# Half of a folded weight product from scaled fp16 parts, and another order of the opening work on all engines

## The reference

```python
def _L0_gnn_ref(feature, graph, weight, wq, wk):
    output = jnp.einsum('bni,io->bno', feature, weight)
    q = jnp.einsum('bni,io->bno', feature, wq)
    k = jnp.einsum('bni,io->bno', feature, wk)
    alpha = jnp.einsum('bno,bmo->bnm', q, k)
    alpha = jnp.maximum(alpha, 0.0) * (graph != 0).astype(alpha.dtype)
    alpha = jax.nn.softmax(alpha, axis=1)
    return jnp.einsum('bnm,bmo->bno', alpha, output)
h = jnp.maximum(_layernorm(x, axis=-1), 0.0)
x = x + _L0_gnn_ref(h, adj, L0_gnn_weight, L0_gnn_wq, L0_gnn_wk)
```

## Time and profile before

| | us |
|---|---|
| median of 3 runs | 412.74 (412.74 to 412.88) |
| profiled execution | 412.91 |
| its span | 411.1 |
| TensorE busy | 405.3 |
| VectorE busy | 298.1 |
| ScalarE busy | 277.7 |
| GpSimd busy | 264.7 |

### The profile page before, as it was taken

The page is one execution under the profiler, slowest core; times in us unless marked ns, Lnnn a source line. Parts: engine busy times, 40 slices in busy tenths (PEclk is TensorE's granted clock), DMA queues, the critical chain, the costliest instruction groups (busy, mean ns, idle before and its releaser), DMA issues.

```text
span 411.1 us, 9529 instructions
## 1 busy us (share of the span) xinstructions
PE 405.3 (99%) x3580; PEld 321.7 (78%) x3580; DVE 298.1 (73%) x571; ACT 277.7 (68%) x592; POOL 264.7 (64%) x286
## 2 busy tenths in 40 slices
PE   8999999999999999999999999999999999999995
PEld 5444545979797997979798897979889797979884
DVE  5797789896867676776767777676777667656565
ACT  4749887765867677766777776776867777644534
POOL 0767896979495866759395775939577584910004
PEclk9999999999999999999999999999999999999999
DMA  8973858989889897997969498985978599493022
GB/s 284 373 110 67 217 103 217 232 205 217 181 208 191 245 155 212 189 204 188 192 212 196 156 214 199 197 218 173 198 241 158 156 220 181 75 197 112 2 104 102
DMA packets 161641, 75.03 MB, mean 183 GB/s; under 512 B 135360, under 2 KB 143808, under 8 KB 161600
## 3 DMA queue, kind: packets, MB, share of 16 engines
q1 hardware_dynamic: 161168, 73.81, 77.6%
q10 hardware_dynamic: 432, 0.66, 0.4%
HBM read 24.12 MB, written 16.78 MB: 99 GB/s over the span
## 4 chain that ended last, share of the span: by engine, by line
PE 90%; DVE 4%; DMA 2%; ACT 1%; SPq 1%; issue 1%; POOL 0%; DVEq 0%; POOLq 0%
PE bank L1166 10%; PE bank L1165 10%; PE bank L1163 10%; PE bank L1181 10%; PE bank L1180 10%; PE bank L1178 10%; PE s_bank L1192 3%; PE s_bank L1193 3%; PE s_bank L1194 3%; PE bank L1199 2%; PE bank L1200 2%; PE bank L1201 2%; PE bank L1320 2%; PE bank L1322 2%; PE bank L1321 2%; DMA x_sb<-in_x 2%
## 5 line engine op out<-in xcount | busy, mean ns | idle before, releaser
L423 POOL TENSOR_TENSOR hn_lo<-h,hn_hi 128x512 f16<-128x512 f32 x64 | 74.0, 1166 | 53.1 <-ACT hn_hi L554 52.9
L544 ACT ACTIVATE h<-x_sb,shift,rstd 128x512 f32<-128x512 f32 x64 | 50.0, 804 | 24.0 <-POOL shift L418 23.6
L449 POOL TENSOR_TENSOR hn_lo<-s,hn_hi 128x512 f16<-128x512 f32 x56 | 63.3, 1163 | 0.3 <-ACT hn_hi L559 0.3
L1163 PE MATMUL bank<-hT_hi,mt_hi 128*128 128x256 f16 x224 | 61.1, 273 | 0.0
L1165 PE MATMUL bank<-hT_lo,mt_hi 128*128 128x256 f16 x224 | 61.1, 273 | 0.0
L1180 PE MATMUL bank<-wt_lo,hT_hi 128*128 128x256 f16 x224 | 61.1, 273 | 0.0
L1166 PE MATMUL bank<-hT_hi,mt_lo 128*128 128x256 f16 x224 | 61.1, 273 | 0.0
L1178 PE MATMUL bank<-wt_hi,hT_hi 128*128 128x256 f16 x224 | 61.1, 273 | 0.0
L1181 PE MATMUL bank<-wt_hi,hT_lo 128*128 128x256 f16 x224 | 61.1, 273 | 0.0
L559 ACT ACTIVATE hn_hi<-s 128x512 f16<-128x512 f32 x56 | 33.8, 625 | 25.6 <-POOL s L438 19.9
L1180 PE MATMUL bank<-w_lo,hT_hi 128*128 128x256 f16 x168 | 45.8, 273 | 0.0
(11 more groups left out here) (169 smaller groups left out, 1115.2 us busy)
## 6 DMA issues: line engine op xcount, KB each, us to landing
out_h<-x_sb SPq DMA_DIRECT2D x63, 256.0 KB, 2.1
x_sb<-in_x SPq DMA_DIRECT2D x15, 1024.0 KB, 5.5
adj_sb<-in_adj SPq DMA_DIRECT2D x16, 256.0 KB, 5.3
hn_hi<-in_L_gnn_wq SPq DMA_DIRECT2D x4, 256.0 KB, 5.6
x_sb<-in_x SPq DMA_DIRECT2D x2, 512.0 KB, 7.2
w_sb<-in_L_gnn_weight SPq DMA_DIRECT2D x2, 512.0 KB, 8.7
hn_lo<-in_L_gnn_wk ACTq DMA_DIRECT2D x2, 256.0 KB, 3.8
hn_lo<-in_L_gnn_wk SPq DMA_DIRECT2D x2, 256.0 KB, 3.7
```

The costliest lines, as they stand in the source:

```text
L423: nc.gpsimd.tensor_tensor(hn_lo[:, s, b], h[:, b], hn_hi[:, s, b], ALU.subtract).then_inc(h_split, 1)
L449: nc.gpsimd.tensor_tensor(low, s32[:, f], high, ALU.subtract).then_inc(s_split, 1)
L544: nc.scalar.activation(h[:, b], x_sb[:, s, b], ACT.Relu, bias=shift[:, b:b + 1], scale=rstd[:, b:b + 1]).then_inc(h_made, 1)
L1163: nc.tensor.matmul(o, bh[:, k, cols], ah[:, :, k], start=first and c == 0 and k == 0, stop=False, skip_group_check=True)
```

## The change

Blocks 2 and 3 of M (`PARTS`) are no longer products in fp32. ScalarE makes the high parts of wk and of the last two blocks of wq, scaled by powers of two from their own maxima; GpSimd makes three of the four low parts of wk from an fp32 copy of the scaled values, VectorE the fourth and those of wq; TensorE multiplies the parts as it does elsewhere. So the maxima of wk, wq and weight are spread one after the other, in three steps each, in place of one spread for all three. v of graphs 0 to 2 is made in another order, part by part, with separate semaphores for the high and low transposes. On ScalarE the exponentials and high parts of p of group 0 go ahead of some high parts of h of group 2; on VectorE the low parts of t (blocks 2 and 3) go ahead of those of `wt`; the statistics and scale blocks of groups 1 and 2 are split or moved; the product with p waits for each graph.

```diff
-    SCALE_STEPS = 7
+    SCALE_STEPS = 12
+    KEY_SCALED, QUERY_SCALED, M_SCALED, W_SCALED = 3, 6, 7, 11
+    PARTS = (2, 3)
...
+        wk_hi, wk_lo = hn_lo[:, 1, 0:K], hn_lo[:, 1, K:2 * K]
+        wk_scaled = spare[:, 0:3].rearrange("p k a d -> p k (a d)")
+        wq_hi, wq_lo = (t[:, 0:2].rearrange("p f a d -> p f (a d)").rearrange("p f (k n) -> p f k n", k=K)
+                        for t in (mt_hi, mt_lo))
...
@@ def _(pool):
+            lo_of_wk(0)
+            lo_of_wk(1)
+            first_scales(0, 0)
+            lo_of_wk(2)
+            first_scales(0, 1)
             for b in range(GB):
                 lo_of_h(0, 0, b)
...
+            first_scales(1, 0)
...
-            layernorm_scales(1)
+            first_scales(1, 1)
             for b in range(GB):
                 lo_of_h(1, 1, b)
+            layernorm_scales(2)
...
-            layernorm_scales(2)
             pool.wait_ge(mt_summed, 3)
...
@@ def _(act):
+            act.wait_ge(scale_step, KEY_SCALED)
+            act.wait_ge(wkT_copied, K)
+            for k in range(K):
+                if k < 3:
+                    nc.scalar.activation(wk_scaled[:, k], wkT[:, k].rearrange("p r n -> p (r n)"), ACT.Copy,
+                                         scale=key_scale).then_inc(wk_scaled_made, 1)
+                nc.scalar.activation(wk_hi[:, k], wkT[:, k].rearrange("p r n -> p (r n)"), ACT.Copy,
+                                     scale=key_scale).then_inc(wk_hi_made, 1)
+            def hi_of_wq(r):
+                act.wait_ge(wqT_filled, r + 1)
+                act.wait_ge(scale_step, QUERY_SCALED)
+                nc.scalar.activation(wq_hi[:, r - 2], wT_bank[r % 2], ACT.Copy, scale=query_scale).then_inc(wq_hi_made, 1)
+            for r in PARTS:
+                hi_of_wq(r)
             for b in range(GB):
                 normalise_h(0, 0, b)
...
-            act.wait_ge(scale_step, 3)
+            act.wait_ge(scale_step, W_SCALED)
             for k in range(K):
...
             normalise_h(2, 2, 2)
+            exponentials(0)
             normalise_h(2, 2, 3)
+            hi_of_p(0)
...
             hi_of_h(2, 0, 2)
             hi_of_h(2, 0, 3)
-            exponentials(0)
-            hi_of_p(0)
...
@@ def _(vec):
+            for r in range(K):
+                key_max(r)
+            top(KEY)
+            query_max(0)
+            top_row(KEY, 0)
+            query_max(1)
+            power(KEY, 0, 0)
+            query_max(2)
+            query_max(3)
+            top(QUERY)
+            stats_first(0)
+            stats_first(1)
+            top_row(QUERY, 1)
+            power(QUERY, 1, KEY_SCALED)
+            stats_first(2)
+            stats_first(3)
+            nc.vector.scalar_tensor_tensor(m_scale[:], key_scale, M_BACK, query_scale, ALU.mult, ALU.mult).then_inc(scale_step, 1)
+            nc.vector.scalar_tensor_tensor(s_unscale[:], pow2[:, QUERY:QUERY + 1], 1.0 / (H_SCALE ** 2 * T_SCALE * m_factor),
+                                           pow2[:, KEY:KEY + 1], ALU.mult, ALU.mult).then_inc(scale_step, 1)
             for k in range(2):
                 vec.wait_ge(w_loaded[k], 16)
+                weight_max(w_sb[:, HK * k:HK * (k + 1)], w_max[:, W, HK * k:HK * (k + 1)])
+            top(W)
+            lo_of_wq(PARTS[0])
+            top_row(W, 2)
+            for r in PARTS[1:]:
+                lo_of_wq(r)
+            power(W, 2, M_SCALED + 1)
+            lo_of_wk(3)
             for k in range(K):
                 vec.wait_ge(w_hi_made, k + 1)
...
+            stats_all(1, 1, 0)
+            stats_all(1, 1, 1)
             for k in range(K):
                 vec.wait_ge(m_hi_made, k + 1)
...
+            stats_all(1, 1, 2)
+            stats_all(1, 1, 3)
...
+            lo_of_whole_t(0, 2)
+            lo_of_whole_t(0, 3)
             lo_of_wt(0)
             lo_of_wt(1)
-            lo_of_whole_t(0, 2)
-            lo_of_whole_t(0, 3)
...
@@ def _(pe):
             transpose_wq(0)
+            spread_top(KEY, 0)
             transpose_wq(1)
-            product_m(0)
+            spread_row(KEY, 0)
+            product_m(0, range(K - 1))
+            spread_top(QUERY, 1)
+            product_m(0, range(K - 1, K))
             transpose_wq(2)
             transpose_wq(3)
-            product_m(1)
...
+            spread_row(QUERY, 1)
+            for c in range(1, PARTS[0]):
+                product_m(c)
+            pe.wait_ge(wk_hi_made, K)
+            for c in PARTS:
+                pe.wait_ge(wq_hi_made, c - PARTS[0] + 1)
+                for k in range(K):
+                    scaled_m(c, wq_hi, wk_hi, k, start=k == 0)
+            spread_top(W, 2)
+            pe.wait_ge(wk_lo_pool, 3)
+            for c in PARTS:
+                for k in range(3):
+                    scaled_m(c, wq_hi, wk_lo, k)
+            spread_row(W, 2)
+            for c in PARTS:
+                pe.wait_ge(wq_lo_made, c - PARTS[0] + 1)
+                for k in range(K):
+                    scaled_m(c, wq_lo, wk_hi, k)
+            pe.wait_ge(wk_lo_vec, 1)
+            for c in PARTS:
+                scaled_m(c, wq_hi, wk_lo, 3, stop=True)
...
+            pe.wait_ge(hT0_hi_landed[0], 16)
+            for k in range(K):
+                pe.wait_ge(w_hi_made, k + 1)
+                first_v(0, hT_hi, w_hi, k, start=k == 0)
...
-            pe.wait_ge(p_split, GB)
             pe.wait_ge(scores_read, 1)
             for b in range(GB):
+                pe.wait_ge(p_split, b + 1)
                 product_out(0, b)
```

More of the change, by code:

```diff
@@ L157, in graph_attention_kernel @@
         shift = sb("shift", [N, GB], F32)
+        W, QUERY, KEY = range(3)
+        w_scale, key_scale, query_scale = (scale_of[:, i:i + 1] for i in (W, KEY, QUERY))
+        m_factor = W_TOP / (4 * D)
+        M_BACK = m_factor / 2.0 ** (2 * W_SHIFT)
         row_max = sb("row_max", [N, GB], F32)
@@ L1303, in product_m, with spread_top, spread_row, scaled_m @@
                     last.then_inc(m_filled, 1)
+            def spread_top(i, n):
+                pe.wait_ge(top_step, 2 * n + 1)
+                nc.tensor.transpose(top_bank[0:1, 0:N], w_top[:, i:i + 1], ident[:]).then_inc(top_filled, 1)
+            def spread_row(i, n):
+                pe.wait_ge(top_step, 2 * n + 2)
+                pe.wait_ge(consts_made, 5)
+                nc.tensor.matmul(top_bank[:, N:N + 1], ones[:], top_col[:, i:i + 1], start=True, stop=True).then_inc(top_filled, 1)
+            def scaled_m(c, left, right, k, start=False, stop=False):
+                mm = nc.tensor.matmul(M_BANK[c], left[:, c - 2, k], right[:, k], start=start, stop=stop)
+                if stop:
+                    mm.then_inc(m_filled, 1)
+            def first_v(b, left, right, k, start=False, stop=False):
+                mm = nc.tensor.matmul(v_bank(0)[b], left[:, 0, b, k], right[:, k], start=start, stop=stop)
+                if stop:
+                    mm.then_inc(whole_v, 1)
             def whole_product_v(g, b):
@@ L1343, in _ @@
-            pe.wait_ge(top_step, 3)
-            pe.wait_ge(consts_made, 5)
-            nc.tensor.matmul(top_bank[:, N:N + 3], ones[:], top_diag[:], start=True, stop=True).then_inc(top_filled, 1)
-            product_m(2, range(1, K))
-            product_m(3)
-            for b in range(GB - 1):
-                pe.wait_ge(hT0_landed[b], 2 * 16)
-                whole_product_v(0, b)
+            spread_row(QUERY, 1)
+            for c in range(1, PARTS[0]):
+                product_m(c)
+            pe.wait_ge(wk_hi_made, K)
@@ new lines, in _ @@
+            pe.wait_ge(wk_lo_vec, 1)
[5 more added lines that the diff above has]
+                first_v(0, hT_hi, w_hi, k, start=k == 0)
+            pe.wait_ge(hT0_lo_landed[0], 16)
+            for k in range(K):
+                first_v(0, hT_lo, w_hi, k)
+            pe.wait_ge(hT0_hi_landed[1], 16)
+            for k in range(K):
+                first_v(1, hT_hi, w_hi, k, start=k == 0)
@@ new lines, in _ @@
+            for k in range(K):
+                pe.wait_ge(w_split, k + 1)
+                first_v(0, hT_hi, w_lo, k, stop=k == K - 1)
+            for k in range(K):
+                first_v(1, hT_hi, w_lo, k)
+            pe.wait_ge(hT0_lo_landed[1], 16)
+            for k in range(K):
+                first_v(1, hT_lo, w_hi, k, stop=k == K - 1)
+            pe.wait_ge(hT0_hi_landed[2], 16)
+            for k in range(K):
+                first_v(2, hT_hi, w_hi, k, start=k == 0)
+            for k in range(K):
+                first_v(2, hT_hi, w_lo, k)
@@ L1353, in _ @@
+            pe.wait_ge(hT0_lo_landed[2], 16)
+            for k in range(K):
+                first_v(2, hT_lo, w_hi, k, stop=k == K - 1)
             pe.wait_ge(m_split, K)
```

167 lines of the change are left out of this document (87 added, 80 removed).

## The result

The change made the kernel slower: 414.04 us (median of 10 runs, 413.74 to 414.46) against 412.75 of the kernel before (10 runs beside them, 412.62 to 413.79), a ratio of 1.0029, 95% interval 1.0021 to 1.0037. Forecast were 411.85 us, with 411.4 to 413.1 as the range. The profiled execution took 413.76 us, its span is 411.9; before it was 412.91 and 411.1.

The account below looks back on a forecast made before the run. TensorE's own stream was taken as the bound, shortenable only up to 31.7 us. M 1.15, fourth product -0.45, vanished wait 0.31 made 1.0, less 0.1 for restarts: 412.74 to 411.85 us, range 411.4 to 413.1.

Parts of the forecast that it names:

- The sum of the head: TensorE's stream up to the first t product: 1.15 - 0.45 + 0.31 = 1.0 us gained, taken as 0.9.
- the fifth transpose: SyncE's transposes of h: the fifth lands at 27.7 us, TensorE asks at 28.1, so hidden by 0.4 us.
- The loss at the fourth product: First v products of graph 0: the fourth waits for ScalarE's high part of w, starting 23.6 not 23.15, 0.45 us lost.
- the 0.1 that I took off for restarts: TensorE's fp16 products behind the spreads of maxima: restarts shown in no row, 0.1 us taken off the 1.0 gain.
- B: Weight's scale on VectorE: one-column operations wait behind GpSimd's low parts of h, t 0.35 us later, 413.1 us; chance 0.15.
- E: SyncE's strict queue: fifth transpose one issue (1.31 us) later, 0.9 not hidden, gain gone, 412.75 us; chance 0.06.
- C: VectorE's two-tensor operations (low part of wk, scalings) miss their turn against GpSimd; gain only 0.3 to 0.6, 412.3 us; chance 0.20.
- D: Weight's spread earlier than listed, high parts of w in time: up to 0.45 us more gain, 411.4 us; chance 0.07.
- Behind it: After the first t product: earlier exponentials keep the 0.9 us gain; h of group 2 some 3 us late, costed at nothing.
- The cover: First product with p, near 57.9 us: moving exponentials ahead saves some 2 us; even half covers the 0.9 us lead.
- The scale block: GpSimd's scale block of group 2 ahead of M's sums: these end up to 1.63 us later; costed nothing, 0 to 0.3 in range.
- My last sentence: If t starts at 30.8 but the span has not shrunk by 0.9, a later wait took the gain; no chance given.

Follow-up runs that it names:

- experiment 5: The changed kernel with group 0's exponentials and GpSimd's scale block of group 2 both moved back to their old places; 412.95 us, ratio 1.0009 to the kernel before.

## Why the prediction was wrong

**The sum of the head was right.** M done at 22.29 (forecast 22.5), the weight's scale at 20.76 (21.0), the fourth v product at 23.41, released by w_hi (23.6), low parts of M in time, the fifth transpose landed at 25.9, ahead of its use at 27.95, and t at 30.54 (30.8). The common 0.2 to 0.3 us is the start: the first product of M at 8.12 (8.46), which is no fixed time: in the profile of experiment 5 it is 8.62. The loss at the fourth product was 0.45 in the forecast; it starts at 23.41 and could at 22.29 + 3 x 0.216 = 22.94, which is 0.47. The head gained 1.09 counted from M's first product, against 0.9; the 0.1 that I took off for restarts was not needed. (One sum was off: 21.0 + 3 x 0.61 + 0.71 is 23.54, not 23.57, which changes nothing.)

**None of the rivals B to E came.** VectorE's timeline of the changed kernel at the weight's scale:

```profile
20.42 0.15 DVE L1070 TENSOR_SCALAR pow<-w_top 128x1 int32<-128x1 int32 x1
20.61 0.15 DVE L1074 TENSOR_SCALAR scale_of<-pow 128x1 int32<-128x1 int32 x1
```

GpSimd made low parts of h meanwhile:

```profile
18.50 3.94 POOL L442 TENSOR_TENSOR hn_lo<-h,hn_hi 128x512 f16<-128x512 f32 x3 [0.30 <-ACT hn_hi L582]
```

An operation on one column of one tensor does not wait for it: 0.15 us, twice, both inside one operation of GpSimd (19.73 to 20.88), where three columns had taken 0.56. The Trainium skill (VectorE: DVE Perf Modes, Mode 2×_2P) asks of an operation that takes both read ports an outermost non-unit dimension that is even, or odd and equal in source and destination. Read strictly, that could cover one column too; the measurement decides against that reading. For C, TensorE has no idle time at 18.31; for D, the high parts of w still came late for the fourth product; for E, see the transpose above.

**The step that failed is "Behind it".** I costed the delay of the high parts of h of group 2 at nothing, since no wait of TensorE stood on it in the earlier trace rows. A table that shows no wait shows no slack either, and its idle time hid the wait of 0.19 us at 57.93. The slack was 0.26 us at the third p product of group 1, in rows that I did not read, and the sum needed two numbers against it: the delay that the move brings (0.87 by then) and the lead itself (1.39), which alone is larger. The delay of h was about what I wrote (3 us, measured 3.1 for the last high parts and 2.0 for the last h), and a part of it was absorbed; it was its price that was wrong: not 0, but 1.8 us when the move was made alone, and 2.0 at the third p product with the lead of the head against it. Without the move the rest of the change takes 411.98 us, close to the 411.85 that I forecast for the whole; but that sum had the scale block's sign wrong too, so its closeness is in part luck.

**The cover was not needed.** I let the move pay for the wait of 57.87 us. In the profile of experiment 5 the exponentials start at 50.77, 0.3 later than before, TensorE is 0.89 early, and the first p product, which now waits for one graph's part and not four, has no wait. The edit of the wait was enough.

**The scale block had the other sign.** I gave it 0 to 0.3 us of loss; it brings 0.8 to 1.2 (0.20 to 0.28%). Without it h of group 2 waits for its shift, on ScalarE ahead of the exponentials. I had looked at what it is moved past, the sums of M, and not at who waits for it.

My last sentence named this outcome, a start of t in time and a span that has not shrunk; no rival carried it, and no part of the range.

## What to carry over

When TensorE has no idle time, ask of each supplier how long before its use it is done; a gain ahead of that point is kept only up to the smallest of these distances, unless the suppliers come earlier too. Compare two timelines from an event that both have (here M's first product) and by starts: the span's first microseconds vary from one execution to the next, and idle time leaves out the overlap that is lost. A step moved ahead on an engine that works in order is priced by two rows: how long its own input is still out (here 1.94 us of standing), and what is queued behind it. Such a move is best tried alone, and a change of several moves one by one: here the gain hangs on one moved call (1.0009 without it), and the whole of the loss on another move.

## What the runs showed of the hardware

A four-column operation of GpSimd took 0.20 us in one order and 1.12 us in another, twice, and ended 0.06 us behind an operation of VectorE on two tensors (0.69 us) that had begun meanwhile; a delay of 0.9 us on the way to all later work came from that one instruction. And four stores of equal size, issued within about 2 us, landed evenly before (the last 3.0 us after its issue), but in the profile of every other kernel here the last one took 4.2 to 5.4 us; the load that waits for it went out later by that. What delays it was not settled.
